# Smaller VectorE steps for the norms, peaks, token factors and first quantisation of a two-layer transformer kernel

## What is computed

```
x = x + xattn0(layernorm(x), ctx)    # 16 heads of 16: causal self-attention plus cross-attention, then @ Wp
x = x + ffn0(layernorm(x))           # per token: rmsnorm, 8-bit rounding, ternary w1, gelu, rmsnorm, rounding, ternary w2
x = x + xattn1(layernorm(x), ctx)    # 16 heads of 16: cross-attention
x = x + ffn1(layernorm(x))           # one 8-bit scale for the whole tensor, before w1 and again before w2
```

## Time and profile before

| | |
|---|---|
| median of 3 runs | 1820.56 us |
| the profiled execution, its own time | 1818.68 us |
| its span, from the first to the last instruction | 1816.7 us |
| TensorE busy | 1616.7 us (89%) |
| VectorE busy | 1410.7 us (78%) |
| ScalarE busy | 1118.6 us (62%) |
| GpSimd busy | 659.2 us (36%) |
| mean granted TensorE clock | 0.951 of full speed |

### The profile page before, as it was taken

One profiled execution on the slowest core, in us unless ns is written; L12 is line 12 of the kernel. 1 busy time (PEld: TensorE's weight loads), 2 busy tenths in 40 slices (PEclk: granted clock), 3 DMA queues, 4 the chain that ended last, 5 costly groups with the idle time before them and its releaser, 6 DMA issues.

```text
span 1816.7 us, 28841 instructions
## 1 busy us (share of the span) xinstructions
PE 1616.7 (89%) x9539; PEld 707.7 (39%) x9552; DVE 1410.7 (78%) x3253; ACT 1118.6 (62%) x2150; POOL 659.2 (36%) x914
## 2 busy tenths in 40 slices
PE   5998889998999989998999999988998997899677
PEld 1344334423443434433443444433443443333236
DVE  5778878778787787778787787878688787787287
ACT  1474475667665675666665675667555855665497
POOL 2436223551454234631454134533561242310140
PEclk7899889999999999999999999999999998999898
DMA  7444313323132323332242323332332231123113
GB/s 188 135 117 120 79 36 100 88 72 98 53 111 78 94 60 100 89 108 62 67 116 60 93 77 91 88 103 73 89 103 59 58 102 44 45 84 133 47 70 117
DMA packets 106947, 159.46 MB, mean 88 GB/s; under 512 B 20656, under 2 KB 83248, under 8 KB 106800
## 3 DMA queue, kind: packets, MB, share of 16 engines
q1 hardware_dynamic: 101208, 155.25, 30.5%
q10 hardware_dynamic: 5592, 2.36, 0.6%
HBM read 105.00 MB, written 51.38 MB: 86 GB/s over the span
## 4 chain that ended last, share of the span: by engine, by line
PE 55%; DVE 23%; ACT 8%; POOL 7%; issue 4%; DMA 2%; ACTq 0%; SPq 0%; DVEq 0%; POOLq 0%
PE acc L1564 12%; PE st L1550 11%; PE misc L1531 10%; DVE nmax L1330 8%; PE misc L1507 7%; PE misc L1479 5%; PE misc L1591 3%; PE misc L1519 3%; DVE misc L1324 3%; ACT tail_h L1110 2%; PE misc L1618 2%; ACT probs L1046 2%; ACT tail_h L1095 1%; PE misc L1605 1%; POOL parts L910 1%
## 5 line engine op out<-in xcount | busy, mean ns | idle before, releaser
L1046 ACT ACTIVATE probs<-st 128x512 f32<-128x512 f32 (+3 forms) x1536 | 758.7, 550 | 392.4 <-PE st L1550 253.9
L1330 DVE TENSOR_REDUCE nmax<-misc 128x1 f32<-128x512 f32 x1024 | 650.9, 683 | 168.9 <-PE misc L1531 165.7
L1531 PE MATMUL misc<-stack 96*128 96x512 bf16 (+3 forms) x1536 | 527.4, 366 | 79.0 <-DVE nmax L1330 46.8
L1550 PE MATMUL st<-stack 99*128 99x512 bf16 (+3 forms) x1536 | 541.6, 364 | 25.0 <-ACT probs L1046 22.7
L1324 DVE CUSTOM_DVE_ANT_0 misc<-misc,mask_mx 128x384 f32<-128x384 f32 (+3 forms) x512 | 239.5, 516 | 78.1 <-PE misc L1531 74.5
L1550 PEld LDWEIGHTS st<-stack 99*128 99x128 bf16 x1536 | 149.1, 99 | 359.0 <-ACT probs L1046 210.9
L1531 PEld LDWEIGHTS misc<-stack 96*128 96x128 bf16 x1536 | 148.0, 100 | 234.1 <-DVE nmax L1330 87.8
L904 POOL TENSOR_TENSOR parts<-qk,zero 128x512 bf16<-128x512 f32 x77 | 80.6, 1046 | 221.0 <-ACT qk L1011 221.0
L1564 PE MATMUL acc<-probs,v_x 128*32 128x512 f32 x1152 | 160.4, 630 | 0.0
L1564 PE MATMUL acc<-probs,v_s 128*32 128x512 f32 (+3 forms) x1152 | 115.4, 473 | 0.1
L916 POOL TENSOR_TENSOR nparts<-nmax,zero 128x16 bf16<-128x16 f32 x96 | 23.7, 247 | 247.3 <-DVE nmax L1330 170.6
(11 more groups left out here) (269 smaller groups left out, 2087.7 us busy)
## 6 DMA issues: line engine op xcount, KB each, us to landing
parts_xk<-parts SPq DMA_DIRECT2D x54, 128.0 KB
stack<-parts_xk SPq DMA_DIRECT2D x36, 192.0 KB, 3.6
parts_xq<-parts SPq DMA_DIRECT2D x51, 128.0 KB
stack<-parts_xq SPq DMA_DIRECT2D x34, 192.0 KB, 3.1
parts_sk<-parts SPq DMA_DIRECT2D x48, 128.0 KB
parts_sq<-parts SPq DMA_DIRECT2D x48, 128.0 KB
stack<-parts_sq SPq DMA_DIRECT2D x32, 192.0 KB, 2.9
stack<-parts_sk SPq DMA_DIRECT2D x32, 192.0 KB, 3.4
```

The lines of the kernel that those rows point to most:

```text
L1046: act.activation(probs[:, j % P_SLOTS, c, T - w:], st_bank(n, 4 * j + c)[:, 0:w], ACT.Exp, scale=SCALE).then_inc(exp_done, 1)
L1330: dve.tensor_reduce(nmax[:, ring, first:first + NT * (len(cs) - 1) + 1:NT], src, AX.X, ALU.max, negate=True).then_inc(misc_free[slot], 1)
L1531: last = pe.matmul(o, stack[0:ROWS, r, 0, c, P * i:P * i + P], stack[0:ROWS, r, 1, c, 0:w], start=True, stop=True)
L1550: last = pe.matmul(o[:, 0:w], stack[0:AUG, r, 1, c, P * j:P * j + P], stack[0:AUG, r, 0, c, T - w:T], start=True, stop=not causal)
```

## The change

Each norm becomes two steps of two instructions, `x_scale` gives its peak to a step `x_peak` of its own, and `quant_x` becomes two steps (the four roundings, then the subtraction). The lists get more cards: `tokens0` and `layer1_norm` one more each, `layer1_last` two, `ffn_norm` 21 instead of 14. GpSimd's bias row after norms F and C goes with the second half. No instruction is added or removed on any engine. Lines below L1243 shift by 4 (L1330 becomes L1334, L1550 becomes L1554).

```diff
 def tokens0(b):
-    return [("ctx_T", b, "A"), ("stats", b, "A"), None, None, ("norm", b, "A"), None, ("norm_T", b, "A"), None]
+    return [("ctx_T", b, "A"), ("stats", b, "A"), None, None, ("norm", b, "A", 0), ("norm", b, "A", 1), None, ("norm_T", b, "A"), None]
...
 def ffn_norm(b):
-    return [("stats", b, "F"), None, None, None, ("norm", b, "F"), ("x_scale", b), ("quant_x", b), None, None, None, None,
-            ("quant_T", b), None, None]
+    return [("stats", b, "F"), None, None, None, ("norm", b, "F", 0), None, ("norm", b, "F", 1), ("x_peak", b), None, None,
+            ("x_scale", b), None, ("quant_x", b, 0), None, ("quant_x", b, 1), None, None, None, ("quant_T", b), None, None]
...
 def layer1_norm(b):
-    return [("stats", b, "C"), None, ("ctx_T", b, "C"), None, None, ("norm", b, "C"), None, ("norm_T", b, "C"), None]
+    return [("stats", b, "C"), None, ("ctx_T", b, "C"), None, None, ("norm", b, "C", 0), ("norm", b, "C", 1), None, ("norm_T", b, "C"), None]
...
 def layer1_last(b):
-    return [("stats", b, "E"), None, None, ("norm", b, "E"), ("finish", b), None, None]
+    return [("stats", b, "E"), None, None, ("norm", b, "E", 0), None, ("norm", b, "E", 1), None, ("finish", b), None]
...
             def norm(s):
-                k = s.args[0]
-                if k in "FC":
+                k, half = s.args
+                if k in "FC" and half:
...
-                for t in range(NT):
+                for t in (2 * half, 2 * half + 1):
...
+            def x_peak(s):
+                dve.wait_ge(xn_done["F"], s.b.times(4, 4).at())
+                dve.tensor_reduce(tok["xmax"][:, :], xn_of(s, "F")[:, :, :], AX.X, ALU.max, apply_absolute_value=True).then_inc(scalars, 1)
+
             def x_scale(s):
                 n = s.b.times(SCALARS)
-                dve.wait_ge(xn_done["F"], s.b.times(4, 4).at())
-                dve.tensor_reduce(tok["xmax"][:, :], xn_of(s, "F")[:, :, :], AX.X, ALU.max, apply_absolute_value=True).then_inc(scalars, 1)
```

More of the change, by code:

```diff
@@ L1253, in quant_x @@
                 n = s.b.times(5)
-                dve.wait_ge(scalars, s.b.times(SCALARS, 6).at())
-                for t in range(NT):
-                    dve.tensor_scalar(xn_of(s, "F")[:, t, :], xn_of(s, "F")[:, t, :], tok["xq"][:, t:t + 1], MAGIC, ALU.mult,
-                                      ALU.add).then_inc(quant, 1)
+                if s.args[0] == 0:
+                    dve.wait_ge(scalars, s.b.times(SCALARS, 6).at())
+                    for t in range(NT):
+                        dve.tensor_scalar(xn_of(s, "F")[:, t, :], xn_of(s, "F")[:, t, :], tok["xq"][:, t:t + 1], MAGIC, ALU.mult,
+                                          ALU.add).then_inc(quant, 1)
+                    return
                 dve.wait_ge(quant, n.at(NT))
@@ L1365, in finish @@
                 dve.tensor_tensor(xrun[:, :], xrun[:, :], xpeak[:, :], ALU.max).then_inc(peak, 1)
-            walk(dve, dict(consts=consts, consts_rest=consts_rest, project=project, split=split, w_peak=w_peak, w_row=w_row, w_tot=w_tot, w_ints=w_ints, stats=stats_, norm=norm, x_scale=x_scale, quant_x=quant_x, hidden=hidden,
+            walk(dve, dict(consts=consts, consts_rest=consts_rest, project=project, split=split, w_peak=w_peak, w_row=w_row, w_tot=w_tot, w_ints=w_ints, stats=stats_, norm=norm, x_peak=x_peak, x_scale=x_scale, quant_x=quant_x, hidden=hidden,
                            hid_peak=hid_peak, hid_scale=hid_scale, down_q=down_q, down=down, v=v, maxima=maxima, heads_out=heads_out,
```

## The result

The changed kernel takes 1804.54 us (median of 5 runs, 1799.26 to 1810.15), the kernel before 1820.56: a ratio of 0.993, 95% interval 0.991 to 0.995. A second series gave 1804.77 against 1817.64, 0.993 (0.991 to 0.995). The change makes the kernel faster by 0.7%, 13 to 16 us and not 35. The profiled execution took 1800.08 us, 18.6 less than the one of before; it is one of the two fastest of its series, whose median is 1804.54.

A forecast was written before the change was run, and what follows sets the result against it. The prediction took TensorE's work plus its waits, chiefly for VectorE's maxima, to bound the kernel. Terms -21.0, -12.6, -1.0, -2.8 and +2.5 sum to -34.9 us, from 1820.6 to 1785.7, stated as 1785; 8-in-10 range 1766 to 1808.

The forecast's parts named there:

- What bounds the kernel: TensorE's own work plus its waits, largest for VectorE's row maxima (46.8 us), with low clock at norm F's long VectorE blocks.
- "-21.0": Norm F, factors and quantisation of batches 1 to 5: shorter blocks save 4.2 of 5.0 us a turn, between -25 and 0.
- "-12.6": Norm F, factors and quantisation of batches 0, 6, 7: 45% of 28.0 us of waits and low clock goes, between -28 and 0.
- "-2.8": Gelu of batch 6: eight maxima instead of two take half of 5.6 us of wait and clock loss, between -5.6 and +1.
- L1237 moved behind the bias row: Batches 0, 6, 7: this 0.17 us instruction, taking up to 2.28 us, surely falls behind GpSimd's bias row.
- "-1.0": Gelu of turns 1 to 4: eight maxima leave; ScalarE gets scores about 3 us sooner; four together -1.0 us, -7.6 to +27.
- "Norms C and E ... nothing": Norms C and E: 1.37 us each, mostly stopping nothing today, covered by TensorE's own work; no time gained or lost.
- "+2.5": Norm A in five turns: second half stands behind one or two more maxima, +0.5 us each, between 0 and +6.
- The signs named beforehand: Profile signs: maxima waits 20 us lower, no 1.8 us wait at norm F; wrong if same-size waits reappear later for other work.
- The waits go and the low clock stays: Rival: throughout the kernel waits fall but low clock moves to other places; 1801.6 us, chance 0.22.
- The lost cover decides: Rival: behind the gelu of turns 1 to 4 eight maxima come on top, up to +27 us; 1831 us, chance 0.08.
- Each added start meets GpSimd: Rival: 48 added VectorE starts, 16 of them blocked by GpSimd, cost 19 us at worst; 1805 us, chance 0.11.

The follow-up runs named there:

- the fourth experiment: The change with five blank cards behind the projection of turns 1 to 5, so norm F's steps go first as before: 1792.03 us, 0.986.
- the ninth experiment: Kernel before with only norm F in pieces and five blank cards behind the projection, so norm F's steps go first: 1790.85 us, 0.986.
- the eighth: Kernel before with four blank cards ending norm F's list in turns 1 to 5, steps whole, projection now ahead of them: 1834.87 us, 1.008.
- the thirteenth: The change with one blank card ahead of the projection beside norm F in turns 1 to 5: 1793.00 us, 0.987.
- the fourteenth experiment: The change with two blank cards ahead of the projection beside norm F in turns 1 to 5: 1804.56 us, 0.994.
- the third experiment: The change's number of cards in every list, but each step whole where its last part stands: 1837.53 us, 1.010 of the kernel before.
- the tenth experiment: The change with norm F's steps first, eight maxima beside the gelu, and norm A whole on its old eight cards: 1779.84 us, 0.980.
- the seventh experiment: The change with norm F's steps first and the next eight maxima, of whichever unit, beside the gelu: 1784.22 us, 0.982.
- The fifteenth experiment: The change with norm F first, eight maxima at the gelu, norm A whole, C and E whole in late turn and last batches' ends: 1783.16 us.

## Why the prediction was wrong in size

The forecast was 1785 us, 35 us less. The measured 1804.5 lies inside the range of 1766 to 1808, but in the part that was given to two rivals, and the gain was 16 us.

**What bounds the kernel** held: maxima, VectorE's long blocks, and a low clock behind them.

**"-21.0" for norm F of batches 1 to 5 is the term that failed.** It measured -3.0. The working stood on the durations of the pieces and on maxima between them, and took for granted that what stands beside norm F stays where it is. With the order kept, the fourth and the ninth experiment measure -17.9 and -18.4 us for the same units: the 4.2 us a turn were 3.6 to 3.7. In turn 2 of the fourth that is 1.9 us of waits (3.2 to 1.3) and 1.8 us of TensorE's busy time (46.5 to 44.7), just what the low clock had been priced at. So the mechanism was right and its size nearly so. The step of the working that failed is that the steps beside norm F keep their order and place: it put the cost of the longer list there at nothing. With the new order 13 to 15 us are gone by the medians (1804.8 against 1792.0, 1805.9 against 1790.9), the waits are back at 3.3 us a turn, and whole steps lose by it too (the eighth). Which single step in that order does it is not shown (the thirteenth and fourteenth). That a list of cards grew from 14 to 21 past one of 17 stood in the diff.

**"-12.6" and "-2.8" for batches 0, 6 and 7** measured -11.1 together. Stretches of the changed kernel, columns as in the earlier trace rows, batches 0, 6 and 7, and the gelu of batch 6:

```profile
205.90:224.80 18.90, 15.55 (x87) 4.66 (x85) 17.57 (x43) 10.62 (x20) 6.60 (x14) 1.00 0.20 49
1357.70:1371.80 14.10, 12.65 (x73) 3.75 (x69) 13.29 (x35) 9.23 (x18) 6.13 (x11) 1.00 0.25 58
1388.20:1412.00 23.80, 17.61 (x88) 7.01 (x86) 16.23 (x51) 19.49 (x32) 2.77 (x9) 0.96 0.14 35
1489.50:1510.30 20.80, 16.30 (x91) 5.42 (x89) 17.99 (x43) 11.55 (x22) 7.48 (x13) 1.00 0.16 40
```

The three units of norm F gain 7.9, 5.5 and 8.5 us (against the 26.8, 19.6 and 29.3 of the earlier trace rows), more than I took, all at full clock (against 0.81, 0.83 and 0.77); I had taken 45% of what was there and 78% came. Their neighbours give half back: the unit of batch 6's gelu takes 23.8 us, for 17.6 before, and TensorE waits there 4.5 us for ScalarE. The term of -2.8 did not come; that unit grew by 6.2. It also holds more matmuls, 88 for 74, so the effect of the eight maxima by themselves is not shown.

L1237 moved behind the bias row as I said. The line over the span, which answers to the earlier trace rows:

```profile
L1237 DVE TENSOR_SCALAR tok_xam<-tok_xam x8: 170/170/171, 216.3 to 1499.6; 128x4 f32<-128x4 f32 x8
```

**"-1.0" for the gelu of turns 1 to 4** measured -9.7 over five units. The gelu's unit and the one behind it, which the term was about, went from 43.1 to 41.4 us a turn, so it was mis-sized: some -6.6 in four turns, near the bright end of its range. The other 3 us are in the last three of the five units, to which I gave nothing: "Norms C and E ... nothing" priced their halves, which indeed bring nothing there (the third experiment), and overlooked that three more cards in the lists move the steps behind them, such as the projection to V from the last place of the fourth unit to the first of the fifth. That is the same oversight as at norm F, here with a gain. ScalarE's side went as forecast, and further. Its timeline at the gelu of turn 2, which answers to the earlier trace rows:

```profile
614.20 3.90 ACT L1068 ACTIVATE hid<-hid 128x1024 f32<-128x1024 f32 x4
618.11 1.28 ACT L1046 ACT_TABLE_LOAD   x1
620.55 0.60 ACT L1046 ACTIVATE probs<-st 128x512 f32<-128x512 f32 x1 [1.16 <-PE st L1554]
```

The 5.78 us of idle time before the table load are 1.16 behind it. The unit that follows is 16.3 us for 15.5, within the 1 us that I allowed.

**"+2.5" for norm A** measured +1.1 in its four units and +0.1 in the second profile, and 4 us by the medians of the tenth experiment. It is small, as I said; its size is not settled.

**The rest**, which I had at nothing, came to +5.8 us in the other units of the late turn.

**The signs named beforehand.** The waits for maxima on the line of 46.8 us fell by 9.5, not by 20, and over all lines they rose. No wait of 1.8 us is left at norm F, the clock there is 1.00, and the 5.0 us at batch 7 are 1.1. But one sign of being wrong did appear: waits "a few places later for other work". The transposes (L1479, now L1483) waited 11.9 us for maxima before and wait 22.4 now.

**The rivals.** *The waits go and the low clock stays* named nearly the time (1801.6), but that is luck, as the opposite happened: the waits for maxima did not fall (76.5 us before, 80.2 after) and the clock rose, by 0.017 in the profile where I said 0.01. *The lost cover decides* did not: the eight maxima cost 3 to 5 us by the units of the seventh experiment, not 27. *Each added start meets GpSimd* (1805) has the time too, and part of its mechanism. The norm's instructions over the span, before and after:

```profile
L1229 DVE TENSOR_SCALAR xn_F<-xmid,mv_F,rstd_F x32: 404/406/409, 212.2 to 1510.5; 128x256 f32<-128x256 f32 x32
```

```profile
L1229 DVE TENSOR_SCALAR xn_F<-xmid,mv_F,rstd_F x32: 396/406/1322, 210.6 to 1495.8; 128x256 f32<-128x256 f32 x32
```

None of the 32 took over 409 ns before; now some take up to 1322. In turn 2 the two long ones end at 563.15 and 564.39 us, each 0.15 us behind an instruction of GpSimd's split (563.00 and 564.24). The Trainium skill (SBUF — State Buffer, "Who interferes with whom") states that a `tensor_scalar` of VectorE in a mode that uses two ports and a GpSimd instruction shut each other out, and the trace agrees. But the norm's longer instructions are not what cost the time. In the fourth experiment three of the four take 0.96 to 1.20 us in each of the five turns, more in sum than in the change, and with one blank card (the thirteenth) one still takes up to 1252 ns; both kernels are 12 us faster than the change.

**What stays open.** F's gain and that of A, C and E do not add: beside F in pieces and in order, A, C and E bring nothing (1790.9 without, 1792.0 with), though in the profiles the gelu's units are 7.5 us shorter there; the late turn's first eight units are 6.4 us longer, its last eight 4.5. TensorE's waits show the same exchange without its reason: with A, C and E in pieces beside F, the waits for maxima are 72.8 us for 58.6, and those for the exponentials 15.6 for 24.0. The fifteenth experiment was to explain that and did not. Open is also why the order costs what it does at norm F.

## What to carry to other kernels

- When a hand-written order is dealt from lists, count the cards: a longer list changes what goes first at every place and where all later steps stand. Here that cost as much as cutting the steps brought at norm F, and it was the whole gain in the units behind the gelu. Try the cards without the pieces before you credit the pieces. Compare the order of both sides on each engine, not only that of the steps that were cut.
- Add up the waits over every line that waits for the same thing before calling a wait gone; and give a kernel's clock and its waits separate terms, as cutting long waits into short ones can give back the clock and leave the waits.
- Take parts of a change one by one on the chip: here two halves of 12 us made 13 together, and the best version (norm F's steps first, eight maxima at the gelu, norm A whole) is at 0.980 (0.977 to 0.982) against the change's 0.993.

## What the runs showed of the hardware

- The sum of TensorE's waits at norm F was 3.2 us before and 3.3 after, in pieces of at most 0.8 us rather than 1.8; the granted clock of the middle unit went from 0.91 to 1.00. But short pieces are no safeguard: in the changed kernel stretches at 1.2 GHz begin at 693, 891 and 1089 us, and the longest wait just ahead of each is 1.3 us.
- A VectorE instruction of 128x256 that takes 0.40 to 0.41 us alone took 0.83 to 1.32 us beside GpSimd's split, in the change and in the fourteenth experiment.
- Stretches at 1.2 GHz differ between executions of one kernel: eleven runs of the change spread from 1799.3 to 1810.2 us, with mean clocks of 0.961 to 0.968. The 0.2% that I took for what can be told apart is too little for single runs, and a difference of 3 us in one unit is not safe from one profile.
